# Attention scores over four banks, a block-diagonal state, and feed-forward units shifted by two, in a one-core transformer block

## The chip, the cores and the metric

The kernel runs on one core of a Trainium2 chip. The metric is device time in microseconds. In what follows PE is TensorE (PEld its weight loads), DVE is VectorE, ACT is ScalarE, POOL is GpSimd and SP is SyncE, which issues most of the transfers.

## The reference

One pre-norm block over 4096 tokens of width 256. Causal linear attention with 16 heads of 16, then a feed-forward part in which every one of 8 experts is computed for every token and weighted:

```python
x = x + attn(layernorm(x))        # q,k,v = x @ w_qkv; rope on q and k; q = elu(q*s)+1, k likewise
#   scan over tokens: kv += k v^T; ks += k; out = (q kv) / max(q . ks, 1e-6); then out @ w_out
x = x + ffn(layernorm(x))
#   inh = sigmoid(x @ Wr / temperature); weights w[token, expert] from it (a zone, else the two nearest)
#   h_e = silu(x @ Wg[e]) * (x @ Wu[e]);  out = sum_e w[:, e] * (h_e @ Wd[e])
```

## The kernel before, in words

Tokens go in 32 tiles of 128. Attention works a tile at a time (g), the feed-forward part a block of four tiles at a time (b, 512 tokens), in 16 units a block: unit n is one half (128 of 256 hidden columns) of one expert, so there are 128 units. To keep fp32 precision most operands are split into a high and a low part, and each product is made of three: hi·hi, hi·lo, lo·hi.

A tile's attention: `qkv` projects; ACT copies (`qk_copy`, `v_copy`); `cos` on DVE, two `sin` on POOL and `rope` make the rotation; `exp` and `phi` the feature map; `q_hi`, `k_hi`, `q_lo`, `k_lo` the split; SP transposes both. `scores(g, half)` makes 8 of the 16 heads' scores: a head takes 64 rows of the array, so an even and an odd head run as a pair into two banks, four heads to a bank. `mask` (DVE, four heads), `a_hi` (ACT) and `a_lo` (POOL) mask and split them; the masked scores have two buffers, so the third mask waits for the first `a_lo`. `av` adds, into two banks (even heads, odd heads), q times the running state (16 products of 64 rows and 51 columns, line 323) and then masked scores times v (32 products of 128 rows, line 330). `o_sum` adds the three parts of each bank, `norm` divides, `state` (line 341) and `st_add` update the running state, which `s1`, `st_rest`, `s2`, `s3` split in three. `o_T` transposes, `proj` projects, `x1_add` adds the residual, `bn2` to `ln2` normalise again, and `x2_T` transposes for the feed-forward part.

A unit: `gate` (6 products of 512 columns, bank G), `silu`, `up` (6, bank U), `h_up`, `h_hi`, `h_lo`, `down` (12 products of 256 columns into Y0 and Y1), and after each second unit four `acc`. Once a block `logit_rows` makes a 16 x 512 array of router rows, `lg_copy` brings it to SBUF, `logit` turns it to 128 x 32 with eight short products against `two` (line 407), and a chain of some 27 small DVE instructions (`route_*`) makes the weights.

The order on every engine is written out by hand: a prologue (tiles 0 to 4, steps 0 to 4), and then a loop over steps s from 5 (LAG). In a step, tile a = s has its `qkv` to `scores`, tile c = s - 1 its `av` to `x2_T`, and four units run, n = 4(s - 5) to n + 3; `down` runs two units later. An engine takes its instructions strictly in this order, and waits are on semaphores. Expert weights come in 24 slabs in the first steps (12 before step 5, four in each of steps 5, 6 and 7), each split by ACT and then by POOL or DVE.

The eight PSUM banks: G, U, Y0, Y1 for the units; R0 for q and k; R1 for v, `x2_T` and the logits; R2 and R3 for scores, then `av`, then `state` and `o_T`, `proj`. Since `scores`, `mask` and `av` share R2 and R3, the second half of the scores waits for the first half's masks.

Of the kernel before, what the change touches and what calls it, by code (L numbers as in the profile page):

```python
# [15 lines left out]
P = 128  # L16
# [22 lines left out]
LAG = 5  # L39
SLABS = 3 * E  # L40
# [3 lines left out]
STEPS = NTL + LAG + 1  # L44
# [24 lines left out]
def build(nc, x, xT, w_qkv, w_out, Wg, Wu, Wd, Wr, temperature, tab, out):  # L69
# [8 lines left out]
    with ctx:  # L78
# [32 lines left out]
        rop = sb("rop", [P, 2 * D])  # L111
# [27 lines left out]
        lg_rows = rt[0:2 * E, :, :, :].rearrange("p i t e -> p (i t e)")  # L139
        two = sb("two", [2 * E, E])  # L140
# [8 lines left out]
            for n in ("gate", "up", "y0", "y1", "front0", "front1", "back0", "back1"))  # L149
# [17 lines left out]
         s_onevx, s_two, s_zsx, s_zss, s_colmean, s_wc, s_wqkv_hi, s_wqkv_lo, s_wout_hi, s_wout_lo, s_wr_hi, s_wr_lo, s_slab_hi,  # L167
         s_slab_lo) = (sem(n) for n in (
             "ones", "mhalf", "mone", "rtemp", "rtemp2", "id0", "mask0", "id", "mask", "iota_i", "iota",
             "z_vx", "one_vx", "two", "z_sx", "z_ss", "colmean", "wc", "wqkv_hi", "wqkv_lo", "wout_hi", "wout_lo", "wr_hi", "wr_lo",  # L170
# [15 lines left out]
        ROUTE = ("inh", "off", "zone", "dist", "zone2", "m", "eq", "w0", "c", "ws", "ix", "no", "s1", "nd",  # L186
# [11 lines left out]
        def score_bank(g, r):  # L198
            return (G, Y1)[r % 2] if g < NT else BK[r % 2]
# [23 lines left out]
        logits = R1[:, D:D + NT * E].rearrange("p (t e) -> p t e", t=NT)  # L223
# [13 lines left out]

        def slab(s, i):

            if s < LAG:  # L240
                n = 3 * s + i
                return n if i < 3 and n < HEAD_SLABS else None
            n = HEAD_SLABS + STEP_SLABS * (s - LAG) + i
            return n if i < STEP_SLABS and n < SLABS else None
# [10 lines left out]
        def tensor_program(pe):  # L255
# [10 lines left out]
            def qkv(g):  # L266
# [23 lines left out]
            def scores(g, half):  # L290
# [5 lines left out]
                if half:  # L296
                    w.wait_ge(s_amask, 4 * g + 2)
                elif g < NT:
                    w.wait_ge(s_amask, 4 * g)
                else:  # L300
                    w.wait_ge(s_ss, 2 * g)
                    w.wait_ge(s_olo, g)
                    if g > NT:
                        w.wait_ge(s_x1, g)
                for j in range(4):
                    for odd in range(2):
                        rows = slice(64 * odd, 64 * odd + 64)
                        m = pe.matmul(score_bank(g, 2 * half + odd)[:, P * j:P * (j + 1)], kT[rows, 4 * half + j, :],  # L308
                                      qT[rows, g % 2, 4 * half + j, :], start=True, stop=True)
                m.then_inc(s_qk, 1)  # L310

            def av(g):
# [4 lines left out]
                w.wait_ge(s_s3, g)  # L317
                w.wait_ge(s_amask, 4 * g + 4)
# [8 lines left out]
                for odd in range(2):  # L327
                    for p in range(NP):
                        for a in a_p:
                            m = pe.matmul(BK[odd][:, p * WV:(p + 1) * WV], a[:, 2 * p + odd, :],  # L330
                                          vx[:, g % 2, 2 * p + odd, :, :].rearrange("p a b -> p (a b)"),
                                          start=False, stop=(p == NP - 1), skip_group_check=True)
                    m.then_inc(s_av, 1)
# [36 lines left out]
            def x2_T(g):  # L370
# [11 lines left out]
            def logit_rows(b):  # L382
# [15 lines left out]
            def logit(b):  # L398
# [59 lines left out]
            state(2); x2_T(1); scores(3, 0); o_T(2); scores(3, 1); proj(2); av(3); x2_T(2); state(3); o_T(3)  # L458
            proj(3); scores(4, 0); x2_T(3); scores(4, 1)
            for s in range(LAG, STEPS):  # L460
                a, c, n = s, s - 1, NT * (s - LAG)
                router = (s - LAG) // NT if (s - LAG) % NT == 0 else -1
                logit_rows(router); gate(n); qkv(a); up(n); logit(router); down(n - 2); av(c); gate(n + 1)
                up(n + 1); down(n - 1); state(c); o_T(c); gate(n + 2); proj(c); up(n + 2); gate(n + 3); down(n)
                scores(a, 0); x2_T(c); up(n + 3); down(n + 1); scores(a, 1)

        def scalar_program(act):
# [41 lines left out]
            def qk_copy(g):  # L509
# [3 lines left out]
                w.wait_ge(s_sin, 2 * g)  # L513
# [11 lines left out]
            def exp(g):  # L525
# [4 lines left out]
                act.activation(qk_bank(g)[:, :], rop[:, :], ACT.Exp, bias=mone[:, 0:1]).then_inc(s_exp, 1)  # L530
# [42 lines left out]
            def s1(g):  # L573
# [5 lines left out]
                act.activation(st_x[:, :, 0, :], st_s[:, :, :], ACT.Copy).then_inc(s_s1, 1)  # L579

            def s2(g):
# [3 lines left out]
                act.activation(st_x[:, :, 1, :], st_r[:, :, :], ACT.Copy).then_inc(s_s2, 1)  # L585
# [16 lines left out]
            def lg_copy(b):  # L602
                if not 0 <= b < NB:
                    return
                w.wait_ge(s_route, routed(b - 1, "wo"))
                w.wait_ge(s_lgrows, b + 1)
                act.activation(lg_rows[:, :], R0[0:2 * E, :], ACT.Copy).then_inc(s_lgc, 1)

            def th(b):
# [3 lines left out]
                w.wait_ge(s_logit, b + 1)  # L613
                act.activation(R["th"], logits, ACT.Tanh, scale=rtemp[:, 0:1]).then_inc(s_th, 1)
# [30 lines left out]
            wout_hi(); slab_hi(0); x_hi(1); qk_copy(0); v_copy(0); load_slab(1); exp(0); v1(0); k_hi(0); q_hi(0)  # L645
            qk_copy(1); v2(0); slab_hi(1); exp(1); slab_hi(2); x_hi(2); q_hi(1); k_hi(1); slab_hi(3); v_copy(1)
            a_hi(0, 0); v1(1); a_hi(0, 1); a_hi(0, 2); a_hi(0, 3); slab_hi(4); qk_copy(2); v2(1); v_copy(2); exp(2)
            s1(0); x_hi(3); v1(2); k_hi(2); q_hi(2); a_hi(1, 0); a_hi(1, 1); s2(0); o_hi(0); a_hi(1, 2); slab_hi(5)
            a_hi(1, 3); x_hi(4); slab_hi(6); qk_copy(3); v2(2); slab_hi(7); v_copy(3); s1(1); a_hi(2, 0); x2_hi(0)
            exp(3); s2(1); v1(3); a_hi(2, 1); o_hi(1); k_hi(3); q_hi(3); a_hi(2, 2); wr_hi(); a_hi(2, 3); v2(3)  # L650
# [628 lines left out]
```

## Time and profile before

| what | value |
|---|---|
| median of three runs | 815.7 us (815.56 to 816.89) |
| profiled execution: time | 815.4 us |
| profiled execution: span, first to last instruction | 813.5 us |
| PE busy | 769.8 us, 95% |
| DVE / ACT / POOL busy | 590.9 / 472.5 / 482.4 us, 73 / 58 / 59% |
| chain that ended last, share of PE | 92% |

Busy PE time counts each product from its start to its modelled end, and ends overlap the next start; the spacing of starts tells what a product costs. In the timeline, equal neighbouring instructions are merged into one row with a count.

### The profile page before, as it was taken

What the parts mean: (1) busy time and instruction counts of PE and PEld (TensorE: products, weight loads), DVE (VectorE), ACT (ScalarE), POOL (GpSimd) and SP (SyncE); (2) the same over time, 40 slices, a digit from 0 to 9 for tenths busy, and PEclk for the clock granted to TensorE, in tenths of its full rate; (3) what the DMA queues carried; (4) which work ended last, traced back from release to release, by engine and by line L of the source; (5) the groups of instructions that cost most, each with busy time, mean ns of one, the idle gap of its engine ahead of it and who ended that gap; (6) DMA issues with size and microseconds to landing.
All of it is one profiled execution on the core that took longest, in us unless ns stands there. A gap on an engine that the chain in (4) does not pass through costs nothing.

```text
span 813.5 us, 18123 instructions
## 1 busy us (share of the span) xinstructions
PE 769.8 (95%) x6696; PEld 658.1 (81%) x6696; DVE 590.9 (73%) x1587; ACT 472.5 (58%) x886; POOL 482.4 (59%) x537
## 2 busy tenths in 40 slices
PE   5375999999999999999999999999999999999997
PEld 3254688888888888888888888888888888888886
DVE  5788688868777787777766787777777787766333
ACT  2674776665656656655666556666656656634222
POOL 2786778755566576655666656565576555652332
PEclk9776899999999999999999999999999999999999
DMA  4545223122211022122201222120121121100000
GB/s 138 126 93 119 59 60 92 39 43 67 41 39 28 16 65 41 40 42 57 43 18 31 43 66 41 39 43 17 50 40 40 41 52 28 27 2 26 2 1 26
DMA packets 97319, 38.27 MB, mean 47 GB/s; under 512 B 74192, under 2 KB 96976, under 8 KB 97232
## 3 DMA queue, kind: packets, MB, share of 16 engines
q1 hardware_dynamic: 90704, 30.83, 17.6%
q10 hardware_dynamic: 6528, 6.29, 2.7%
q8 instruction: 53, 0.87, 0.4%
q14 instruction: 34, 0.28, 0.1%
HBM read 16.13 MB, written 4.19 MB: 25 GB/s over the span
## 4 chain that ended last, share of the span: by engine, by line
PE 92%; DVE 4%; ACT 1%; issue 1%; POOL 1%; DMA 0%; ACTq 0%; DVEq 0%; POOLq 0%
PE y L448 22%; PE gate L415 22%; PE up L415 22%; PE front L285 6%; PE back L330 3%; PE front L286 3%; PE back L366 2%; PE back L308 2%; PE back L341 2%; PE front L379 1%; PE back L353 1%; PE front L393 1%; PE back L323 1%; PE front L407 1%; POOL a_lo L1121 1%
## 5 line engine op out<-in xcount | busy, mean ns | idle before, releaser
L1149 POOL TENSOR_TENSOR h_lo<-work,h_hi 128x512 fp32r<-128x512 f32 x128 | 165.7, 1295 | 176.3 <-ACT h_hi L641 176.3
L1121 POOL TENSOR_TENSOR a_lo<-am,a_hi 128x512 f16<-128x512 f32 x120 | 140.2, 1180 | 67.4 <-ACT a_hi L570 67.1
L448 PE MATMUL y<-wd_hi,h_hi 128*128 128x256 f32 x512 | 145.0, 283 | 1.1 <-DVE xa L1024 1.1
L448 PE MATMUL y<-wd_lo,h_hi 128*128 128x256 f32 x512 | 143.0, 279 | 0.0
L448 PE MATMUL y<-wd_hi,h_lo 128*128 128x256 f32 x512 | 142.9, 279 | 0.0
L634 ACT ACTIVATE work<-gate 128x512 f32<-128x512 f32 x128 | 75.6, 591 | 81.4 <-PE gate L415 81.1
L1024 DVE SCALAR_TENSOR_TENSOR xa<-y,wo,xa 128x256 f32<-128x256 f32 x256 | 115.8, 471 | 7.8 <-PE y L448 7.6
L1012 DVE TENSOR_TENSOR work<-work,up 128x512 f32<-128x512 f32 x128 | 87.0, 680 | 36.2 <-PE up L415 31.8
L641 ACT ACTIVATE h_hi<-work 128x512 fp32r<-128x512 f32 x128 | 80.1, 626 | 48.5 <-DVE work L1012 31.6
L448 PEld LDWEIGHTS y<-wd_hi,h_hi 128*128 128x128 f32 x512 | 96.2, 188 | 8.2 <-issue 2.7
L797 DVE TENSOR_TENSOR am<-back,cmask 128x512 f32<-128x512 f32 x112 | 74.3, 684 | 38.0 <-PE back L308 37.9
L448 PEld LDWEIGHTS y<-wd_lo,h_hi 128*128 128x128 f32 x512 | 96.2, 188 | 4.7
L448 PEld LDWEIGHTS y<-wd_hi,h_lo 128*128 128x128 f32 x512 | 97.2, 190 | 0.0
L570 ACT ACTIVATE a_hi<-am 128x512 f16<-128x512 f32 x120 | 74.4, 628 | 35.3 <-DVE am L797 32.9
L415 PE MATMUL gate<-x_hi,wg_hi 128*128 128x512 f32 x256 | 87.7, 424 | 0.0
L415 PE MATMUL up<-x_hi,wu_hi 128*128 128x512 f32 x256 | 82.1, 402 | 0.0
L415 PE MATMUL gate<-x_hi,wg_lo 128*128 128x512 f32 x256 | 80.0, 394 | 0.0
L415 PE MATMUL up<-x_hi,wu_lo 128*128 128x512 f32 x256 | 79.7, 393 | 0.0
L415 PE MATMUL up<-x_lo,wu_hi 128*128 128x512 f32 x256 | 79.7, 392 | 0.0
L415 PE MATMUL gate<-x_lo,wg_hi 128*128 128x512 f32 x256 | 79.4, 391 | 0.0
L1100 POOL TENSOR_TENSOR rop<-qk,tabs 128x256 f32<-128x256 f32 x64 | 45.3, 728 | 25.3 <-ACT qk L515 25.3
L415 PEld LDWEIGHTS gate<-x_hi,wg_lo 128*128 128x128 f32 x256 | 48.4, 189 | 11.6
(194 smaller groups left out, 1654.1 us busy)
## 6 DMA issues: line engine op xcount, KB each, us to landing
xr<-xT SPq DMA_DIRECT2D x32, 128.0 KB, 2.5
xa<-x SPq DMA_DIRECT2D x32, 128.0 KB, 2.6
out<-xa SPq DMA_DIRECT2D x32, 128.0 KB, 1.8
xa<-Wg ACTq DMA_DIRECT2D x8, 256.0 KB, 2.9
work<-Wd ACTq DMA_DIRECT2D x8, 256.0 KB, 3.0
work<-Wu ACTq DMA_DIRECT2D x8, 256.0 KB, 2.9
work<-w_qkv SPq DMA_DIRECT2D x2, 384.0 KB, 3.7
qT<-q_st SPq DMA_TRANSPOSE x32, 3.2
```

Of the source, the lines that this page charges most:

```text
L285: pe.matmul(qk_bank(g)[:, :], lhs, wqkv_p[wi][:, k, 0:2 * D], start=first, stop=last)
L415: m = pe.matmul(ps, weights[wi][:, e_, k, m_ * P:(m_ + 1) * P], x2[xi][:, b % 2, k, :], start=(n == 0), stop=(n == 3 * KD - 1))
L448: m = pe.matmul(Y[t // 2][:, t % 2 * D:(t % 2 + 1) * D], h_p[hi][:, n % 2, t * P:(t + 1) * P], wd_p[wi][:, u // KI, u % KI, :], start=(n % ...
L570: act.activation(a_p[0][:, heads(r), :], am_place(g, r).rearrange("p (h n) -> p h n", h=4), ACT.Copy).then_inc(s_ahi, 1)
L634: act.activation(hb[:, n % 2, :], G[:, :], ACT.Silu).then_inc(s_g, 1)
L641: act.activation(h_p[0][:, n % 2, :], hb[:, n % 2, :], ACT.Copy).then_inc(s_hhi, 1)
L797: v.tensor_tensor(am_place(g, r).rearrange("p (h n) -> p h n", h=4), score_bank(g, r)[:, :].rearrange("p (h n) -> p h n", h=4), bcast(cmas ...
L1012: v.tensor_tensor(hb[:, n % 2, :], hb[:, n % 2, :], U[:, :], ALU.mult).then_inc(s_h, 1)
L1024: v.scalar_tensor_tensor(out=xs, in0=Y[t // 2][:, t % 2 * D:(t % 2 + 1) * D], scalar=wo[:, b % 2, t, e_:e_ + 1], in1=xs, op0=ALU.mult, op1 ...
L1100: pool.tensor_tensor(r2_h[:, :, half, :], qk_h[:, :, 1 - half, :], bcast(tabs[:, g // NT % 2, g % NT, at:at + HALF], 1, 2 * H), ALU.mult). ...
L1121: pool.tensor_tensor(a_p[1][:, heads(r), :], am_place(g, r).rearrange("p (h n) -> p h n", h=4), a_p[0][:, heads(r), :], ALU.subtract).then ...
L1149: pool.tensor_tensor(h_p[1][:, n % 2, :], hb[:, n % 2, :], h_p[0][:, n % 2, :].bitcast(F32), ALU.subtract).then_inc(s_hlo, 1)
```

## The change

- The scores of a tile use four banks, R0 to R3, and both halves run in one group. So `qkv(a)` of the next step waits for the first two masks, and `x2_T` moves one step later (to tile d = s - 2), between `up(n)` and `av(c)`.
- The units of a step are n = 4(s - 5) - 2 to n + 3: two fewer have run at a given tile. Steps 5, 6 and 7 are written out by hand (with ten units), the loop begins at step 8, and there is one more step at the end.
- The running state is kept block-diagonal by pairs of heads (its other blocks are zero, by a per-partition scale `own`), so q times the state is eight products of 128 rows and 102 columns. The state's buffers, and what `s1`, `st_rest`, `s2` and `s3` handle, have 272 columns for 136.
- `logit` is four transposes through the identity for eight products against `two`, and a new `route_sum` on DVE adds the two parts. `logit_rows` and `logit` go later in the step; the small routing instructions are split over two steps.
- `rope` writes over `qk`, so `qk_copy` waits for the `phi` of the tile before; the prologue's order is changed on all engines.

```diff
-            return (G, Y1)[r % 2] if g < NT else BK[r % 2]
+            return (G, Y1)[r % 2] if g < NT else (R0, R1, R2, R3)[r]
...
                 for p in range(NP):
-                    for odd in range(2):
-                        rows = slice(64 * odd, 64 * odd + 64)
-                        pe.matmul(BK[odd][:, p * WV:(p + 1) * WV], qT[rows, g % 2, p, :],
-                                  st_x[rows, p, :, :].rearrange("p a b -> p (a b)"),
-                                  start=(p == 0), stop=False, skip_group_check=True)
+                    pe.matmul(BK[p // 4][:, p % 4 * 2 * WV:(p % 4 + 1) * 2 * WV], qT[:, g % 2, p, :],
+                              st_x[:, p, :, :, :].rearrange("p h a b -> p (h a b)"),
+                              start=(p % 4 == 0), stop=False, skip_group_check=True)
...
                 for t in range(NT):
-                    m = pe.matmul(logits[:, t, :], lg_rows[:, t * P:(t + 1) * P], two[:, :], start=(t == 0),
-                                  stop=(t == NT - 1), skip_group_check=True)
+                    m = pe.transpose(R1[:, t * P:(t + 1) * P], lg_rows[:, t * P:(t + 1) * P], ident[:, :])
...
-            proj(3); scores(4, 0); x2_T(3); scores(4, 1)
-            for s in range(LAG, STEPS):
-                a, c, n = s, s - 1, NT * (s - LAG)
+            proj(3); scores(4, 0); scores(4, 1); x2_T(3); qkv(5); gate(0); av(4); up(0); o_T(4); state(4)
+            logit_rows(0); proj(4); gate(1); logit(0); scores(5, 0); gate(2); up(1); scores(5, 1); qkv(6); gate(3)
...
+            for s in range(FULL, STEPS):
+                a, c, d, n = s, s - 1, s - 2, NT * (s - LAG) - 2
                 router = (s - LAG) // NT if (s - LAG) % NT == 0 else -1
-                logit_rows(router); gate(n); qkv(a); up(n); logit(router); down(n - 2); av(c); gate(n + 1)
-                up(n + 1); down(n - 1); state(c); o_T(c); gate(n + 2); proj(c); up(n + 2); gate(n + 3); down(n)
-                scores(a, 0); x2_T(c); up(n + 3); down(n + 1); scores(a, 1)
+                qkv(a); gate(n); up(n); x2_T(d); av(c); gate(n + 1); down(n - 2); up(n + 1); state(c); o_T(c)
+                gate(n + 2); down(n - 1); proj(c); logit_rows(router); gate(n + 3); up(n + 2); logit(router)
+                down(n); scores(a, 0); scores(a, 1); up(n + 3); down(n + 1)
...
+                v.scalar_tensor_tensor(out=st_s[:, :, hh, :], in0=stp[:, :, hh, :], scalar=own[:, hh:hh + 1],
+                                       in1=st_s[:, :, hh, :], op0=ALU.mult, op1=ALU.add).then_inc(s_ss, 1)
...
+            def route_sum(b):
...
+                v.tensor_reduce(R["s2"], logits, AX.X, ALU.add).then_inc(s_route, 1)
```

The loop on DVE and ACT after the change, cut to what the prediction follows:

```diff
+                tcos_scale(a); mask(c, 2); route_first(late); mask(c, 3); acc(n - 4, 0); bn(a + 1); acc(n - 4, 1)
+                acc(n - 4, 2); acc(n - 4, 3); mean_var(a + 1); cos(a); route_second(late); o_sum(c, 0); rope(a)
+                x2_lo(d); o_sum(c, 1); h_up(n); den_max(c); den_rec(c); phi(a); var_eps(a + 1); route_tie(late)
+                norm(c); route_ix2(late); x_lo(a + 1); route_s2(late); k_lo(a); q_lo(a); o_lo(c); st_add(c)
...
+                acc(n - 2, 2); acc(n - 2, 3); bn2(c); mean_var2(c); var_eps2(c); h_up(n + 2); route_sum(router)
+                ln2(c); route_zone(router); route_nearest(router); route_weight(router); mask(a, 0); mask(a, 1)
+                h_up(n + 3)
...
+                a_hi(c, 2); x_hi(a + 1); a_hi(c, 3); v_copy(a); qk_copy(a); silu(n); h_hi(n - 1); x2_hi(d); exp(a)
+                silu(n + 1); k_hi(a); q_hi(a); h_hi(n); o_hi(c); v1(a); silu(n + 2); h_hi(n + 1); lg_copy(router)
+                s1(c); silu(n + 3); v2(a); th(router); s2(c); e1(router); h_hi(n + 2); fb(router); a_hi(a, 0)
```

## Rows read from the trace of the kernel before

**Rows 1.** The page: busy time by engine, and the chain that ended last.
```profile
PE 769.8 (95%) x6696; PEld 658.1 (81%) x6696; DVE 590.9 (73%) x1587; ACT 472.5 (58%) x886; POOL 482.4 (59%) x537
PE 92%; DVE 4%; ACT 1%; issue 1%; POOL 1%; DMA 0%; ACTq 0%; DVEq 0%; POOLq 0%
```

**Rows 2.** Windows: stretch, its length, busy us (instructions) by engine, granted clock, DMA share, GB/s.
```profile
0.00:100.00 100.00, 61.62 (x611) 46.51 (x612) 74.42 (x199) 58.02 (x117) 64.21 (x83) 0.78 0.44 106
...
100.00:125.00 25.00, 25.00 (x218) 21.61 (x217) 22.05 (x61) 17.36 (x33) 19.08 (x22) 1.00 0.40 87
...
300.00:400.00 100.00, 100.00 (x915) 86.26 (x914) 75.64 (x206) 62.05 (x114) 61.28 (x70) 1.00 0.18 39
```

**Rows 3.** Timeline of PE: start us, us, what; first product of qkv in two steps.
```profile
390.64 0.39 PE L285 MATMUL front<-wqkv_hi,xo_hi 128*128 128x512 f32 x1
...
413.56 0.39 PE L285 MATMUL front<-wqkv_hi,xo_hi 128*128 128x512 f32 x1
```

**Rows 4.** Timeline of PE: last product of down, av, first of gate.
```profile
395.42 0.28 PE L448 MATMUL y<-wd_hi,h_lo 128*128 128x256 f32 x1
395.63 0.38 PE L323 MATMUL back<-st_x,qT 64*128 64x51 bf16 x16
395.95 0.20 PE L330 MATMUL back<-vx,a_hi 128*128 128x51 bf16 x1
...
396.77 0.71 PE L415 MATMUL gate<-x_hi,wg_hi 128*128 128x512 f32 x2
```

**Rows 5.** Timeline of PE: last product of down, then state.
```profile
400.89 0.28 PE L448 MATMUL y<-wd_hi,h_lo 128*128 128x256 f32 x1
401.00 0.77 PE L341 MATMUL back<-vx,k_st 128*128 128x34 bf16 x24
```

**Rows 6.** Timeline of PE: x2_T into up; down into scores into gate.
```profile
408.56 0.44 PE L379 MATMUL front<-ident,nat 128*128 128x128 f32 x2
408.76 0.71 PE L415 MATMUL up<-x_hi,wu_hi 128*128 128x512 f32 x2
409.31 0.63 PE L415 MATMUL up<-x_hi,wu_lo 128*128 128x512 f32 x2
...
411.53 0.28 PE L448 MATMUL y<-wd_hi,h_lo 128*128 128x256 f32 x1
411.74 0.40 PE L308 MATMUL back<-qT,kT 64*128 64x128 f16 x8
412.07 0.74 PE L415 MATMUL gate<-x_hi,wg_hi 128*128 128x512 f32 x2
412.64 0.62 PE L415 MATMUL gate<-x_hi,wg_lo 128*128 128x512 f32 x2
413.10 0.62 PE L415 MATMUL gate<-x_lo,wg_hi 128*128 128x512 f32 x2
```

**Rows 7.** Timeline of PE in a router step: logit, then down.
```profile
369.90 1.05 PE L407 MATMUL front<-two,router 16*128 16x8 f32 x8
370.89 0.38 PE L448 MATMUL y<-wd_hi,h_hi 128*128 128x256 f32 x1
```

**Rows 8.** Timeline of all engines: masks, a_hi, a_lo and h_up.
```profile
408.75 1.29 DVE L797 TENSOR_TENSOR am<-back,cmask 128x512 f32<-128x512 f32 x2 [0.95 <-PE back L308]
...
409.47 1.23 ACT L570 ACTIVATE a_hi<-am 128x512 f16<-128x512 f32 x2
...
410.18 2.29 POOL L1121 TENSOR_TENSOR a_lo<-am,a_hi 128x512 f16<-128x512 f32 x2 [1.86 <-ACT a_hi L570]
...
410.50 0.69 DVE L1012 TENSOR_TENSOR work<-work,up 128x512 f32<-128x512 f32 x1
```

**Rows 9.** Timeline of DVE: rope, the two o_sum, after the av of rows 4.
```profile
395.79 0.69 DVE L772 SCALAR_TENSOR_TENSOR rop<-front,rop 128x512 f32<-128x512 f32 x1 [0.25 <-POOL rop L1100]
396.63 1.07 DVE L815 TENSOR_REDUCE osb<-back 128x136 f32<-128x408 f32 x2 [0.15 <-PE back L330]
```

**Rows 10.** Timeline of ACT: a table load ahead of exp.
```profile
394.42 1.28 ACT L530 ACT_TABLE_LOAD   x1
```

More of the change, by code:

```diff
@@ L612, in th @@
                 w.wait_ge(s_rtemp2, 1)
[L613 to L614 removed]
+                w.wait_ge(s_route, routed(b, "sum"))
+                act.activation(R["th"], R["s2"], ACT.Tanh, scale=rtemp[:, 0:1]).then_inc(s_th, 1)
             def e1(b):
@@ L654, in scalar_program @@
[L654 to L661 removed]
+            wout_hi(); x_hi(1); load_slab(1); slab_hi(0); qk_copy(0); v_copy(0); slab_hi(1); x_hi(2); v1(0); exp(0)
@@ L669, in setup_first @@
                 v.memset(mone[:, :], -1.0).then_inc(s_mone, 1)
+                for hh in range(2):
+                    for half in range(2):
+                        v.memset(own[64 * half:64 * half + 64, hh:hh + 1], ASCALE if half == hh else 0.0).then_inc(s_own, 1)
                 w.wait_ge(s_iota_i, 1)
@@ new lines, in vector_program @@
+            wout_lo(); tcos_scale(0); cos(0); rope(0); x_lo(1); phi(0); x_lo(2); tcos_scale(1); q_lo(0); k_lo(0)
+            slab_lo(2); rtemp_half(); cos(1); rope(1); phi(1); tcos_scale(2); mask(0, 0); mask(0, 1); q_lo(1)
+            mask(0, 2); k_lo(1); mask(0, 3); cos(2); o_sum(0, 0); o_sum(0, 1); rope(2); mask(1, 0); tcos_scale(3)
+            den_max(0); phi(2); st_add(0); den_rec(0); mask(1, 1); norm(0); x_lo(3); mask(1, 2); q_lo(2); k_lo(2)
+            mask(1, 3); o_lo(0); slab_lo(5); x1_add(0); bn2(0); cos(3); o_sum(1, 0); mean_var2(0); bn(4)
@@ new lines, in vector_program @@
+            var_eps2(0); o_sum(1, 1); mean_var(4); mask(2, 0); rope(3); den_max(1); ln2(0); den_rec(1); mask(2, 1)
+            norm(1); x_lo(4); wr_lo(); var_eps(4); phi(3); mask(2, 2); st_add(1); q_lo(3); tcos_scale(4); k_lo(3)
+            mask(2, 3); x2_lo(0); o_lo(1); cos(4); x1_add(1); slab_lo(8); bn2(1); o_sum(2, 0); o_sum(2, 1)
+            mean_var2(1); var_eps2(1); den_max(2); mask(3, 0); ln2(1); den_rec(2); st_add(2); norm(2); mask(3, 1)
+            x2_lo(1); rope(4); o_lo(2); mask(3, 2); mask(3, 3); phi(4); bn(5); x1_add(2); mean_var(5); bn2(2)
@@ new lines, in vector_program @@
+            mean_var2(2); var_eps2(2); k_lo(4); q_lo(4); o_sum(3, 0); ln2(2); o_sum(3, 1); den_max(3); den_rec(3)
+            norm(3); x_lo(5); x2_lo(2); o_lo(3); st_add(3); var_eps(5); x1_add(3); bn2(3); mean_var2(3); var_eps2(3)
+            mask(4, 0); tcos_scale(5); ln2(3); mask(4, 1); slab_lo(11); mask(4, 2); x2_lo(3); bn(6); mask(4, 3)
+            mean_var(6); cos(5); rope(5); phi(5); o_sum(4, 0); o_sum(4, 1); den_max(4); den_rec(4); slab_lo(14)
+            norm(4); q_lo(5); k_lo(5); o_lo(4); h_up(0); x1_add(4); bn2(4); x_lo(6); mean_var2(4); st_add(4)
@@ new lines, in vector_program @@
+            route_sum(0); var_eps2(4); slab_lo(17); var_eps(6); mask(5, 0); route_zone(0); mask(5, 1)
+            route_nearest(0); mask(5, 2); h_up(1); mask(5, 3); bn(7); route_weight(0); route_first(0); tcos_scale(6)
+            ln2(4); slab_lo(20); cos(6); o_sum(5, 0); h_up(2); rope(6); o_sum(5, 1); route_second(0); den_max(5)
+            mean_var(7); phi(6); den_rec(5); x2_lo(4); norm(5); x_lo(7); route_tie(0); h_up(3); route_ix2(0)
+            o_lo(5); q_lo(6); route_s2(0); k_lo(6); route_both(0); x1_add(5); route_out(0); var_eps(7); bn2(5)
@@ new lines, in vector_program @@
+            acc(0, 0); mean_var2(5); acc(0, 1); acc(0, 2); acc(0, 3); var_eps2(5); h_up(4); st_add(5); mask(6, 0)
+            mask(6, 1); h_up(5); mask(6, 2); ln2(5); tcos_scale(7); mask(6, 3); cos(7); acc(2, 0); acc(2, 1)
+            rope(7); acc(2, 2); h_up(6); acc(2, 3); o_sum(6, 0); bn(8); o_sum(6, 1); phi(7); mean_var(8); den_max(6)
+            acc(4, 0); den_rec(6); norm(6); q_lo(7); h_up(7); k_lo(7); slab_lo(23); o_lo(6); acc(4, 1); acc(4, 2)
+            acc(4, 3); st_add(6); var_eps(8); h_up(8); x1_add(6); x2_lo(5); mask(7, 0); bn2(6); mean_var2(6)
```

214 lines of the change are left out of this document (100 added, 114 removed).

## The prediction

> **What bounds the kernel now.** I read the page first: PE is busy for 95% of the span, and 92% of the chain that ended last is PE's own work [rows 1]. Then the windows: from 100 us on PE is busy in every microsecond at the full clock (1.00, 2.4 GHz), while DVE has 76% and ACT and POOL about 62% in the middle of the run; in the first 100 us PE is busy for only 61.6 us at a mean clock of 0.78 [rows 2]. So there are two regimes. After the prologue the time is the sum of what PE issues, and work taken from another engine is worth nothing; a step lasts 413.56 - 390.64 = 22.92 us [rows 3]. In the prologue PE waits for the others. "Busy" hides PE's small losses, as products overlap in the record. The timeline shows them as spacings: a pair of 512-column products takes 0.46 us (412.64 to 413.10), 0.23 each [rows 6], and a down product is normally followed after 0.11 to 0.12 us [rows 5].
>
> **The change part by part, on PE.**
>
> *Entries.* Where down is followed by 64-row products the spacing is 0.21 us in place of 0.12: before the state products of av [rows 4] and before each half of the scores [rows 6]. Before `state`, which has 128 rows and the same type as av's products, it is 0.11, so nothing is lost [rows 5]. The change makes av's first products 128-row ones (0.09 gone) and puts both halves of the scores in one group (another 0.09).
>
> The Trainium skill's page "TensorEngine Tiling (Array Packing)", section Key Properties, says that a change of the tiling mode, not of the tile, drains the engine; by this rule, the trace agrees: these 0.09 us are that drain, and they stand only before 64-row groups.
>
> *Exits.* After a group of short products the first pair of 512-column ones takes longer, their weights not being loaded under anything: 0.57 against 0.46 after scores, 0.55 after x2_T [rows 6]. With one group of scores one exit goes (0.11), and with x2_T put just before av, which ends in such an exit anyway, another goes (0.09).
>
> *State products.* Sixteen take 395.95 - 395.63 = 0.32 us [rows 4]. At one column a cycle of 2.4 GHz eight of 102 columns take 8 x 0.0425 = 0.34; I take +0.05 with the entry from x2_T. Bounds: the 32 v products behind them go at (396.77 - 395.95) / 32 = 0.026 us each [rows 4]; if the wide ones went so too, 0.21, a gain of 0.11. A product of x2_T takes 0.10 [rows 6]; at that price 0.80, a loss of 0.48 a tile.
>
> The same page, section Performance Considerations, wants two-way row tiling for a contraction of 64 or less, which speaks against this edit: two tiles side by side would take 51 columns a pair, 8 x 0.021 = 0.17 us (an estimate from its rule), and undoing them would cost 0.17 a tile, 5.4 us over 32. The row says 0.32 before, 0.04 a pair, so the pairs do not get their columns for half; the row decides.
>
> Sum for a tile: -0.09 - 0.09 - 0.11 - 0.09 + 0.05 = -0.33. Tiles 4 to 31 are in the PE-bound part: 28 x 0.33 = 9.2 us.
>
> *Router.* Eight products against `two` last 370.89 - 369.90 = 0.99 us [rows 7], with a drained entry (they have 16 rows; I take the 0.09 of rows 4). Four transposes of x2_T's kind take 4 x 0.10 = 0.40 [rows 6]; the exit stays. -0.68 a block, eight blocks: 5.4 us. Bounds: 4 x 0.09 above, and nothing gained below, if a transpose took the 0.25 of two such products.
>
> **Waits, one step of the new order.** They are what can eat this. Let T be the start of the scores; widths from rows 4, 6, 8 and 9.
>
> *Masks to av.* Mask 0 starts at T + 0.5, as before [rows 6, 8], a mask each 0.64, a_hi 0.62, a_lo 1.14: a_lo 0 ends at 3.1, a_lo 1 at 4.2. The third and fourth mask wait for these two buffers, so mask 3 ends at 4.9, its a_hi at 5.5; POOL has `s3` (0.44 in the old width, I take double) and a_lo 2 until 6.1, and a_lo 3 until 7.3. PE comes to av after scores 0.65, up 1.5, down 1.4, qkv 6 x 0.23 + 6 x 0.12 = 2.1, gate and up 2.8, x2_T 0.2: T + 8.6. Spare: 1.3 us. qkv at T + 3.6 waits for masks 0 and 1, done at 1.9: spare 1.7.
>
> *av to up(n+1).* Queued on DVE are o_sum 0, rope, x2_lo, o_sum 1, h_up. With A the start of av: o_sum 0 at A + 1.0 (396.63 - 395.63) [rows 4, 9], 0.53 each, rope 0.62, x2_lo some 0.4 (half of h_up's columns), h_up 0.65: A + 3.7. PE is at up(n+1) at A + 1.14 + gate 1.5 + down 1.4 = 4.0. Spare: 0.3 us, the smallest of all. norm, behind phi, ends at A + 5.2, and o_T comes at 6.1.
>
> *Router steps.* The routing stands in front of the masks: route_sum 0.7 us after up(n+2) ends, tanh, then e1 behind a table load of 1.28 us [rows 10], so that mask 0 starts some 3.4 us after up(n+2), 1.0 later than the scores would allow. It leaves 0.3 of the 1.3. And exp is called between two silu, so two more loads, 2.6 us of ACT, one of them before silu(n); gate(n+1) has about 0.9 us for that. I take 0 and keep 1 us a block as a bound.
>
> The Trainium skill's page "ScalarE: Activation LUTs", section "Table sets: the hidden batching unit", puts a load at about 2.7 us (its section on the cost itself at 1.28); at 2.7 silu(n) would come 1.4 later and a router step stall by half a microsecond or more. The row of this case, 1.28, decides.
>
> *The wider state.* s1, s2, st_rest, s3 handle twice the columns: at most double, under 1 us together, with 14 us between `state` and the av that needs them. st_add has as many columns as before over more partitions. route_sum and the second half of the routing lie in DVE's free quarter. All at nothing; if that cover went, DVE would be the bound and each would count.
>
> **Prologue and steps 5 to 7.** Here PE is not alone. qkv(5) now runs before the router rows of block 0, in a gap, worth up to 1 us. But ten units are run by step 8 for twelve. The three steps, 68.8 us now, hold six groups of 1.4 us less (two gates, ups and downs) and savings of 1.7, and the router rows of block 0 (0.9) come in: about 59.5 us of PE. DVE had between 76% (an ordinary step) and 88% (22.05 of 25 us) of such a time [rows 2], 52 to 60 us; less two h_up and four acc, 3 us, it is 49 to 57 us for PE's 59.5, 83 to 97%. ACT and POOL have the slabs on top too. With every engine so full PE must wait somewhere. Whatever is lost here is paid in full, as the two postponed units run at the end. I take +3.4 us, bounds -2 and +9. Tiles 0 to 3 are reordered on all engines with the same work; DVE carries 74 of the first 100 us [rows 2]. I take 0, bounds -4 and +4.
>
> **Sum.** -9.2 - 5.4 + 3.4 = -11.2 us. The profiled execution took 815.4 us, span 813.5, within 0.3 of the median of 815.7, so the sum is made on the median: 804.5 us.
>
> **The rivals.**
>
> *A. The head eats more.* Steps 0 to 7 lose 9 us for 3.4. For: the loads above, and 38 us of PE idle before 100 us, where any order matters. Against: PE hardly idled after 100 us although DVE was at 88%. 810.
>
> *B. The small losses move and do not vanish.* Entries and exits turn out to be per group of products whatever their rows, and the wide products cost 0.1 more than thought: tile gain 0.1, 2.8 us, router 5.4, head +3.4. For: x2_T to av is a pair that the trace never shows. Against: rows 5. 811.
>
> *C. Router steps stall.* e1 and the added loads hold masks and silu up past their spare, 1.5 us in each of seven blocks: +10.5. For: DVE waits for ACT there with the masks behind it. Against: the spares. 815, no change.
>
> *D. Slower: up(n+1) waits for h_up(n) in every step.* DVE's five instructions between av and up have 0.3 us to spare. If x2_lo waits for x2_hi (behind a_hi, two copies, silu and h_hi on ACT), or rope for sin, DVE stops with h_up behind it and PE with it. Beyond 0.3 us late each 0.1 costs 2.8 us over 28 tiles; it decides from 0.3 + 11.2 / 28 = 0.7 us late. At 1.2 late: 28 x 0.9 = 25, so 829. For: a DVE at three quarters has only a quarter to catch up with. Against: x2_T ends at A and DVE comes to x2_lo only at A + 2.1; the sins start when qk is copied, long before.
>
> **How the numbers follow.** Forecast 0.60, A 0.14, B 0.10, C 0.07, D 0.09. A measurement of this kernel tells 0.2%, 1.6 us, from no change. Forecast, A and B are faster, and a little of C: 0.86; same 0.04 (C); slower 0.10 (D and C's tail). The forecast's own range is 799 to 808 (bounds of wide products, router and head); with A, B and most of C it is 797 to 815.
>
> **What would show it.** In the trace after: av's first eight products start 0.1 after x2_T's last and take 0.34 to 0.36; one group of 16 score products in 0.65; the transposes of the logits in 0.4; steps of 22.6 us with no PE idle in the middle; idle of PE between 80 and 140 us some 4 us. Wrong would be: PE idle before up, av or gate in every step (D, C), a step still near 22.9 (B), or PE idle for over 8 us between 80 and 140 us (A).

## The result, and the profile after

The changed kernel takes 828.3 us (827.4 to 829.2, four runs) against 815.6 us (815.1 to 816.9) for the kernel before: ratio 1.0153, interval 1.0135 to 1.0171. It is slower by 12.7 us, where 804.5 was forecast and 797 to 815 was the range. The profiled execution took 827.7 us, its span 826.0.

The page of the changed kernel, busy time and chain, answers to [rows 1]:

```profile
PE 771.7 (93%) x6408; PEld 661.0 (80%) x6408; DVE 613.3 (74%) x1598; ACT 504.5 (61%) x898; POOL 494.2 (60%) x538
PE 81%; POOL 5%; DVE 4%; ACT 4%; issue 3%; DMA 2%; SPq 0%; ACTq 0%; DVEq 0%; POOLq 0%
```

PE issues 288 products fewer and is busy for longer. The windows of [rows 2]:

```profile
0.00:100.00 100.00, 61.03 (x549) 46.37 (x550) 73.77 (x185) 56.04 (x112) 66.78 (x84) 0.73 0.44 110
100.00:125.00 25.00, 18.94 (x139) 15.05 (x137) 20.19 (x53) 17.39 (x30) 14.43 (x16) 0.93 0.26 69
300.00:400.00 100.00, 99.03 (x864) 85.79 (x863) 80.43 (x217) 68.50 (x120) 64.25 (x71) 1.00 0.19 39
```

From 100 to 125 us, where PE had no gap before, it is now busy for 18.9 of 25 us. From 80 to 140 us it is busy for 48.0 of 60 us (57.0 before): 12 us idle, where the forecast named 4 and its rival A over 8. In the middle it is nearly full again. The two timelines of PE that the forecast rested on, scores and x2_T to av, answer to [rows 4, 6]; the first row is the last down product ahead of the scores:

```profile
411.70 0.27 PE L436 MATMUL y<-wd_hi,h_lo 128*128 128x256 f32 x1
411.91 0.40 PE L302 MATMUL front<-qT,kT 64*128 64x128 f16 x8
412.14 0.39 PE L302 MATMUL back<-qT,kT 64*128 64x128 f16 x8
412.46 0.73 PE L403 MATMUL up<-x_hi,wu_hi 128*128 128x512 f32 x2
413.03 0.63 PE L403 MATMUL up<-x_hi,wu_lo 128*128 128x512 f32 x2
413.50 0.63 PE L403 MATMUL up<-x_lo,wu_hi 128*128 128x512 f32 x2
...
420.30 0.38 PE L371 MATMUL front<-ident,nat 128*128 128x128 f32 x2
420.51 0.54 PE L316 MATMUL back<-st_x,qT 128*128 128x102 bf16 x8
420.89 0.18 PE L323 MATMUL back<-vx,a_hi 128*128 128x51 bf16 x1
...
421.72 0.71 PE L403 MATMUL gate<-x_hi,wg_hi 128*128 128x512 f32 x2
```

The structure is the forecast's: one group of scores, entered after 0.21 us and 0.55 long (0.65 was forecast); the wide state products 0.38 long; no gap before av. But the pairs of 512-column products stand 0.47 apart, not 0.46. Averaged from 160 to 700 us, the spacing of such pairs is 0.4664 us (0.4599 before) and that of down products 0.1194 (0.1166). Nothing in the code of those products was changed.

The first `qkv` product of two steps, for [rows 3]; the step between them, 23.53 us, is the one behind a router step:

```profile
391.87 0.39 PE L276 MATMUL front<-wqkv_hi,xo_hi 128*128 128x512 f32 x1
...
415.40 0.40 PE L276 MATMUL front<-wqkv_hi,xo_hi 128*128 128x512 f32 x1
```

Ordinary steps take 22.85 us (22.92 was forecast to become 22.6), a block of four 93.4 (93.8). PE's waits from 150 to 740 us (what waited, for what; us, times, longest), of which there were none before, and the largest of those from 60 to 160 us:

```profile
PE gate L403 <- ACT work L628: 2.9, 6, 0.5
PE back L323 <- POOL a_lo L1142: 0.4, 1, 0.4
...
PE y L371 <- DVE nat L895: 4.3, 3, 3.1
PE back L323 <- POOL a_lo L1142: 3.7, 3, 1.6
PE gate L403 <- ACT work L628: 3.1, 2, 2.8
PE y L359 <- DVE ox_lo L859: 2.7, 3, 1.1
PE front L302 <- DMA kT<-k_st: 1.9, 1, 1.9
```

Divided at the first product of `qkv(8)` and of `qkv(31)`, in us; what lies before `qkv(8)` is called the head below. At `qkv(8)` the changed kernel has run seven groups (gate, up or down of a unit) fewer, 1.4 us each; I count these 9.8 us, which fall behind `qkv(31)`, to the head:

| stretch | forecast | changed less before |
|---|---|---|
| to qkv(8) (155.1, now 158.0) | +1.4 | 2.9 + 9.8 = +12.7 |
| 23 steps (539.8, now 537.6) | -11.7 | -2.2 |
| tail (118.6, now 130.4) | -1.0 | 11.8 - 9.8 = +2.0 |
| span (813.5, now 826.0) | -11.3 | +12.5 |

The forecast's column is its own terms laid out: four tiles, a router and the 3.4 in the first stretch, 23 tiles and six routers in the second, one of each in the tail.

Both large terms are off: 11 us in the head, 12.5 in everything after it.

### The profile page after: what moved, and what is told of

It reads as the page before. It is cut to its first block, busy times and chain, and to the rows that moved or that the text cites. A ratio compares the mean times of both kernels' runs of the same rounds, so it can differ in the third digit from the quotient of the medians.

```text
span 826.0 us, 17554 instructions
## 1 busy us (share of the span) xinstructions
PE 771.7 (93%) x6408; PEld 661.0 (80%) x6408; DVE 613.3 (74%) x1598; ACT 504.5 (61%) x898; POOL 494.2 (60%) x538
## 4 chain that ended last, share of the span: by engine, by line
PE 81%; POOL 5%; DVE 4%; ACT 4%; issue 3%; DMA 2%; SPq 0%; ACTq 0%; DVEq 0%; POOLq 0%
PE y L436 21%; PE gate L403 21%; PE up L403 20%; PE front L276 5%; POOL a_lo L1142 3%; PE back L323 3%; PE front L277 2%; PE back L359 2%; PE back L334 2%; DMA kT<-k_st 1%; PE front L302 1%; PE back L346 1%; PE back L316 1%; PE front L384 1%; ACT qk L508 1%
## 5 line engine op out<-in xcount | busy, mean ns | idle before, releaser
L1031 DVE SCALAR_TENSOR_TENSOR xa<-y,wo,xa 128x256 f32<-128x256 f32 x256 | 109.9, 474 | 30.1 <-PE y L436 30.1
L403 PE MATMUL gate<-x_hi,wg_hi 128*128 128x512 f32 x256 | 85.8, 416 | 6.6 <-ACT work L628 6.6
L816 DVE TENSOR_REDUCE osb<-back 128x136 f32<-128x408 f32 x64 | 36.7, 575 | 34.0 <-PE back L323 34.0
L403 PEld LDWEIGHTS gate<-x_lo,wg_hi 128*128 128x128 f32 x256 | 48.3, 189 | 11.8
```

Of the source, the lines that this page charges most:

```text
L403: m = pe.matmul(ps, weights[wi][:, e_, k, m_ * P:(m_ + 1) * P], x2[xi][:, b % 2, k, :], start=(n == 0), stop=(n == 3 * KD - 1))
L816: v.tensor_reduce(osb[:, 8 * half:8 * half + 8, :], BK[half][:, 0:8 * WV].rearrange("p (h s d) -> p h d s", s=3, d=W1), AX.X, ALU.add).the ...
L1031: v.scalar_tensor_tensor(out=xs, in0=Y[t // 2][:, t % 2 * D:(t % 2 + 1) * D], scalar=wo[:, b % 2, t, e_:e_ + 1], in1=xs, op0=ALU.mult, op1 ...
```

## Experiments

Theory: the head pays for the postponed units in full, and the middle loses its gain because products are issued at a wider spacing, x2 (what gate and up read) and h (what down reads) standing at other addresses (x2 at 193216 bytes of a partition for 193344, h at 220320 for 220480). Rival for the middle: the new order itself. First the kernel before again, for a second trace, beside the changed kernel with its old addresses, one part alone, and all parts without the shift.

> The kernel before, unchanged, traced again, to compare product spacings. Between the two traces gate and up pairs of 512 columns went from 0.460 to about 0.467 us and down products from 0.1184 to 0.1199 (means). Placement theory: this kernel has 0.460 and 0.118 again, on whichever chip. Chip theory: it shows 0.467 and 0.120 where a copy of the changed kernel would.

816.9 us, span 815.1; `qkv(5)` at 87.7 and `qkv(8)` at 156.6 (86.3 and 155.1 in the first trace), so single traces differ by 1.5 us in the head, and ordinary steps by nothing (22.8 to 22.9 in both). Its pairs are 0.460 apart and its down products 0.117, as in the first trace, so the wider spacing isn't a matter of which execution was traced.

**e1_pad: the changed kernel, x2 and h at the addresses of before.**

```diff
-        own = sb("own", [P, 2])
+        own = sb("own", [P, 34])
...
+        gap = sb("gap", [P, 8])
         wo = sb("wo", [P, 2, NT, E])
```

> The changed kernel with 128 unused bytes per partition ahead of xa and 32 ahead of wo, so that xa, x2, the router array, work and h lie at the addresses of the kernel before; order and work unchanged. Placement theory: pairs return to 0.460 and down products to 0.118; 768 pairs x 0.0065 + 1536 x 0.0015 = 7 us less than 828.3, so 821 (ratio to before about 1.007). Rival (chip, or the new order itself): spacing stays at 0.467 and 0.120, ratio 1.015.

821.4 us, ratio 1.0060 (1.0046 to 1.0075): 6.9 us less than the changed kernel (7.6 by the ratios), with not one instruction changed. Its gate and up rows at the same place as above are 0.46 apart:

```profile
412.96 0.62 PE L404 MATMUL gate<-x_hi,wg_hi 128*128 128x512 f32 x2
413.42 0.62 PE L404 MATMUL gate<-x_hi,wg_lo 128*128 128x512 f32 x2
413.88 0.62 PE L404 MATMUL gate<-x_lo,wg_hi 128*128 128x512 f32 x2
414.34 0.62 PE L404 MATMUL up<-x_hi,wu_hi 128*128 128x512 f32 x2
```

Ordinary steps take 22.59: the gain of a tile, 0.29, was there and had been covered. The new order as the cause of the wide spacing is out. A block gains 1.33, not 4 x 0.33 + 0.68; the wait of gate for silu stands in its trace too (3.5 us in six steps, each the one behind a router step).

**e2_logit: the transposed logits and route_sum in the kernel before, nothing else.**

```diff
-                    m = pe.matmul(logits[:, t, :], lg_rows[:, t * P:(t + 1) * P], two[:, :], start=(t == 0),
-                                  stop=(t == NT - 1), skip_group_check=True)
+                    m = pe.transpose(R1[:, t * P:(t + 1) * P], lg_rows[:, t * P:(t + 1) * P], ident[:, :])
```

> The kernel before with one part of the change: logits by four transposes and a route_sum, in the place where logit stood. Step theory (each edit is worth what I forecast, the loss is in the order of the first eight steps): logit takes 0.4 for 0.99 us and a drained entry, 8 x 0.68 = 5.4 us, so 810.3. Rival (the routing chain is what counts): the extra DVE instruction ahead of tanh delays exp or h_up, and the gain stays under 2 us: 814.

811.5 us, ratio 0.9938 (0.9926 to 0.9950), -5.1 by the ratio; a router step takes 23.54 for 24.31. The size was right.

**e3_all and e4_parts: all parts but the shift, in two orders.** Logits, block-diagonal state and scores over four banks. In e3 `logit_rows` runs in the step before and the whole routing stands ahead of `x2_lo`:

```diff
+                route_s2(router); route_both(router); route_out(router); x2_lo(c)
+                slab_lo(slab(s, 3)); h_up(n + 3); mask(a, 0); mask(a, 1)
```

> The kernel before, its prologue, its units (not shifted) and its order, with all three parts on PE: transposed logits, block-diagonal state, both score halves in one group over R0 to R3; x2_T stays in its step, ahead of up(n+3), and buffers lie as before. Theory 1 (the loss is in the prologue and steps 5 to 7): per tile -0.09 -0.09 -0.11 +0.05 = -0.24, 28 tiles 6.7 us, router 5.4, the head as before: 815.6 - 12 = 804, range 801 to 808. Theory 2 (one score group over four banks makes the steps wait: masks to av has little to spare): PE idle before av or qkv in every step, 815 or more.

822.9 us, ratio 1.0079 (1.0066 to 1.0092): a miss by 19 us. Ordinary steps took 22.57, router steps 25.4 for 24.3. PE's waits from 150 to 740 us name it:

```profile
PE front L412 <- ACT vs L534: 5.6, 6, 0.9
PE front L382 <- DVE router L1004: 2.8, 6, 0.5
PE front L313 <- DVE x_lo L919: 1.0, 6, 0.2
```

`logit` waited for v's copy out of the bank that they share, `x2_T` for routing. In e4 the rows go to bank U at the start of the step, and `route_both` and `route_out` come last:

```diff
+                route_s2(router); x2_lo(c); h_up(n + 3); mask(a, 0); mask(a, 1)
+                slab_lo(slab(s, 3)); route_both(router); route_out(router)
```

> The three parts again on the prologue, units and buffers of the kernel before, with the routing mended: the router rows go to bank U at the start of the step (free there), so no score group waits for them, and x2_lo and the masks stand ahead of the last routing instructions. In the run e3_all the ordinary steps were 22.57 us for 22.86 of before and the router steps 25.4 for 24.3. Parts theory (the edits are worth 0.3 a tile and 4.3 us of routing; the changed kernel lost them elsewhere): 815.7 - 28 x 0.3 - 4.3 = 803. Rival (four banks for one tile's scores cost waits whatever the order): PE idle in router steps stays, 812 or more.

809.8 us, ratio 0.9914 (0.9901 to 0.9928). Ordinary steps take 22.57; the expectation of 803 missed 0.4 us in each step behind a router step (down for acc, which waits for the late `route_out`: 1.4 us in 7 in its trace) and 2.7 in the head.

**e5_shift: e4 with the units shifted by two**, stores and loads as in the changed kernel.

```diff
-SHIFT = 0
+SHIFT = -2
...
-                a, c, n = s, s - 1, NT * (s - LAG)
+                a, c, n = s, s - 1, NT * (s - LAG) + SHIFT
```

> e4_parts with one thing more: the units of a step are n = 4(s-5)-2 to n+3 from step 5 on, and one more step at the end; the order in a step, the prologue and the buffers are those of e4_parts. Shift theory: in steps 5 to 7 the kernel before had little PE idle, so two units (8.4 us of gate, up and down) put off there are paid in full at the end: e4_parts + 6 to 8.5. Order theory (the hand-written order of steps 5 to 7 is what costs): the shift alone costs under 3 us.

819.4 us, ratio 1.0035 (1.0022 to 1.0047). By the medians the shift alone costs 9.65 us, no less than two units at the end. The two traced executions differ by only 6.6 us (e4's lies 2.6 above its median): there e5 comes to `qkv(8)` 1.9 us earlier, with 8.4 us of units not yet run. So the head gives back little or nothing. From 60 to 160 us, e4 and then e5 (for the kernel before the same window has 88.73 of PE, for the changed one 81.75):

```profile
60.00:160.00 100.00, 88.25 (x781) 73.83 (x780) 77.52 (x207) 64.42 (x122) 74.22 (x79) 0.87 0.36 78
```

```profile
60.00:160.00 100.00, 82.63 (x739) 68.07 (x738) 78.95 (x205) 61.21 (x119) 72.00 (x77) 0.86 0.34 77
```

PE does 5.6 us less in the same time, while DVE is busy for 77.5 and 79.0. In e5 two of PE's waits in that window have grown, `av` for a_lo from 1.4 us and `state` for o_sum from 0.8:

```profile
PE back L330 <- POOL a_lo L1134: 3.3, 2, 1.9
PE back L341 <- DVE osb L821: 3.0, 2, 2.1
```

The granted clock is lower in the head too, which the forecast didn't count. From 60 to 120 us it is 0.83 of 2.4 GHz in the kernel before and 0.74 in the changed one (0.78 in e4, 0.77 in e5):

```profile
60.00:120.00 60.00, 48.73 (x510) 39.07 (x501) 48.06 (x139) 39.50 (x77) 42.91 (x48) 0.83 0.35 84
```

```profile
60.00:120.00 60.00, 41.92 (x401) 32.57 (x402) 45.63 (x110) 35.04 (x69) 43.13 (x47) 0.74 0.38 94
```

In the changed kernel the clock even falls once more after it had come up: PE was busy for 15.15 of the 24 us from 89 to 113, waited 2.85 us for a silu, and then had 0.51 of the clock from 113.0 to 116.4. Over the whole head (to `qkv(8)`), 44.4 and 51.2 us lie at 1.2 GHz in the two traces of the kernel before, 54.6 in e4, and 58.0 in each of e5, e1_pad and the changed kernel. What this costs, no run separates. The two traces of the kernel before are 6.8 us apart in it and 1.5 us apart at `qkv(8)`; at that rate (an estimate) the 7 to 14 us more of the changed kernel are 1.5 to 3 us of its head.

**e7_state: the block-diagonal state alone, in the kernel before.**

```diff
-                    for odd in range(2):
-                        rows = slice(64 * odd, 64 * odd + 64)
-                        pe.matmul(BK[odd][:, p * WV:(p + 1) * WV], qT[rows, g % 2, p, :],
+                    pe.matmul(BK[p // 4][:, p % 4 * 2 * WV:(p % 4 + 1) * 2 * WV], qT[:, g % 2, p, :],
```

> The kernel before with the block-diagonal state alone (rope into qk, wider st_s, st_r, st_x; addresses from xa on unchanged). av's first eight products take 0.38 us for sixteen in 0.32, with the entry of 0.21 us back at 0.12: 32 x -0.03 = -1 us, 814.7. Rival: the wider s1, st_rest, s2, s3 and the qk buffer shared with rope slow the prologue, where the others bound: 817 or more.

816.8 us, ratio 0.9999 (0.9990 to 1.0008): no change, where 1 us less was expected.

**Addresses, in the kernel before.** Six runs move buffers and change no instruction. e6: 32 unused bytes ahead of wo. e8: den and rec (128 bytes) go from ahead of nat to behind h. e11: to behind x2. e12, e13: 128 and 256 unused bytes ahead of nat. e14: 128 ahead of wo. The edits are of this kind (e8, e14):

```diff
-        den = sb("den", [P, H])
-        rec = sb("rec", [P, H])
...
         h_p = [sb(f"h_{s}", [P, 2, B], F32R) for s in ("hi", "lo")]
+        den = sb("den", [P, H])
+        rec = sb("rec", [P, H])
```

```diff
+        gap = sb("gap", [P, 32])
         wo = sb("wo", [P, 2, NT, E])
```

> The kernel before with 32 unused bytes per partition ahead of wo, so that work and h (not x2) lie 32 bytes further, as h does modulo 64 in the changed kernel. Placement theory, the part of h: down products go from 0.118 to 0.120 and gate and up stay at 0.460; +2 to +4 us, 818 to 819. If the whole effect sits in x2, or in distances other than modulo 64: no change, 815.7.

> The kernel before with one edit: the two small buffers den and rec (128 bytes a partition together) are allocated behind h in place of ahead of nat, so that everything from nat to h stands 128 bytes lower: x2 exactly where the changed kernel has it, h still on a multiple of 64 bytes. No instruction changes. Theory (the spacing of products depends on the address of their operand, x2's for gate and up, h's for down): pairs of gate and up 0.466 us for 0.460 in the middle of the run, down products unchanged at 0.116 to 0.117, and with 768 pairs (128 units, 6 pairs each) about +4 to +5 us, ratio 1.005. Rival (only the 32-byte offset of h and its neighbours matters, or what was seen in the changed kernel is owed to its order): 816, pairs 0.460.

> The kernel before with den and rec allocated right behind x2: x2 (and what stands between nat and it) 128 bytes lower, at 193216, work and h where they were. Theory (each product's spacing depends on the address of its own operand): pairs of gate and up 0.466 us as in the run with everything 128 bytes lower, down products back at 0.1166 (there 0.1179); 768 pairs at +0.006 = +4.6 us less what is idle anyway: about 820. Rival (what counts is h's or work's address, or the mere sum of what moved): pairs 0.460 and 816, or pairs and down both slow and 821.

> The kernel before with an unused buffer of 128 bytes ahead of nat: x2 at 193472, h at 220608, both 128 bytes higher. If the pattern of fast and slow addresses repeats every 256 bytes, this is the same as 128 bytes lower: pairs 0.466, down 0.118, about 821. If only the distance or the order counts (lower is slow, higher not): 816 and 0.460.

> The same with 256 bytes: x2 at 193600, h at 220736. If the pattern repeats every 256 bytes: pairs 0.460, down 0.1166, 816, as the kernel before. If every other address than that of before is slow: 821.

> The kernel before with 128 unused bytes ahead of wo: wo, work and h 128 bytes higher (h at 220608), x2 where it was. With x2 alone lower by 128, the pairs went to 0.4665 and the down products to 0.1148. If the pairs follow x2's own address and the down products the distance between x2 and h (odd in units of 128 bytes is good): pairs 0.460, down 0.115, 1536 x 0.0017 = 2.6 us less: about 814, ratio 0.997. Rival (down follows h's own address, 220608 as in the run with everything 128 bytes higher): down 0.118 and 818 to 819, pairs 0.460.

Bytes moved, mean spacing of pairs of gate and up and of down products between 160 and 700 us (some 320 and 990 of them each), ratio to the kernel before with interval:

| run | x2 | h | pair | down | ratio |
|---|---|---|---|---|---|
| before | 0 | 0 | 0.4599 | 0.1166 | 1 |
| e6_align | 0 | +32 | 0.4592 | 0.1182 | 1.0025 (1.0015, 1.0036) |
| e14_h128 | 0 | +128 | 0.4610 | 0.1178 | 1.0019 (1.0010, 1.0028) |
| e11_x2only | -128 | 0 | 0.4666 | 0.1148 | 0.9997 (0.9988, 1.0006) |
| e8_x2addr | -128 | -128 | 0.4666 | 0.1179 | 1.0052 (1.0038, 1.0066) |
| e12_g128 | +128 | +128 | 0.4666 | 0.1179 | 1.0062 (1.0049, 1.0076) |
| e13_g256 | +256 | +256 | 0.4609 | 0.1164 | 1.0001 (0.9992, 1.0010) |
| changed | -128 | -160 | 0.4664 | 0.1194 | |
| e1_pad | 0 | 0 | 0.4613 | 0.1156 | |

With x2 the buffers from nat on move too, and with h wo and work; but of these the pairs read x2 alone, and the down products h. The pairs are at 0.459 to 0.461 with x2 at 0 and +256, at 0.4665 with it at -128 and +128, wherever h is. The down products are slow with h moved by 32 or 128, and as before at 256. The expectation of e14, that the distance of the two decides, fell, its rival held. Two more missed: e8's down products were to stay as they were, and e11 was to cost 4 us. In e11 the down products are quicker than ever, and over the 20 steps behind `qkv(8)` they give back 1.7 of the 2.1 us that gate and up lose; why is not settled. Nor is h's address all that sets the down products: with x2 and h where they stood, they take 0.1156 in e1_pad and 0.1157 in e10, for 0.1166 before. The rows of e11's pairs, and of e14's:

```profile
412.53 0.63 PE L415 MATMUL gate<-x_hi,wg_lo 128*128 128x512 f32 x2
413.00 0.63 PE L415 MATMUL gate<-x_lo,wg_hi 128*128 128x512 f32 x2
413.46 0.39 PE L285 MATMUL front<-wqkv_hi,xo_hi 128*128 128x512 f32 x1
```

```profile
415.16 0.63 PE L416 MATMUL gate<-x_hi,wg_lo 128*128 128x512 f32 x2
415.63 0.62 PE L416 MATMUL gate<-x_lo,wg_hi 128*128 128x512 f32 x2
```

One row tells little at a resolution of 0.01; the mean over hundreds does, and the modelled durations (0.62 or 0.63) show nothing.

**A version that beats both.** e4's parts, with the first half of the routing back ahead of `x2_lo`; e9 leaves the block-diagonal state out, e10 has it, e15 is e10 with h 128 bytes higher.

```diff
-                route_s2(router); x2_lo(c); h_up(n + 3); mask(a, 0); mask(a, 1)
-                slab_lo(slab(s, 3)); route_both(router); route_out(router)
+                route_s2(router); route_both(router); x2_lo(c); h_up(n + 3); mask(a, 0); mask(a, 1)
+                slab_lo(slab(s, 3)); route_out(router)
```

> Meant to beat both kernels: the kernel before with transposed logits and four-bank scores, without the block-diagonal state and without the shift; on DVE the first half of the routing stays ahead of x2_lo, h_up(n+3) and the masks, and route_out comes after the masks. From earlier runs: an ordinary step gains 0.3 (of that 0.09 was to come from av's entry, which stays, and 0.05 is not paid), router 4.35, the prologue pays nothing as the state edit that made qkv(5) a microsecond later is out. 28 x 0.25 + 4.35 = 11: about 806. Rival (the 0.3 of a tile needs the state edit): 816 - 4.35 - 28 x 0.15 = 808. Rival (the late route_out holds acc and down in the step after a router step, 0.4 each as in the version with all three parts, and the head loses 2.7 as there): 811.

> The same with the block-diagonal state as well: differs from the version of the three parts run earlier only in that the first half of the routing is ahead of x2_lo. If the wait of that version (down for acc for route_out) goes: 809.8 - 7 x 0.4 = 807, ordinary steps 22.57. Beside e9 it says what the state edit is worth in this order: the forecast's terms give -0.09 + 0.05 a tile, 28 x 0.04 = -1.1; alone it gave 0. Rival (state costs a microsecond in the prologue): e9 + 1.

> The fastest version so far (transposed logits, four-bank scores, block-diagonal state, no shift; 0.9872 of before) with the same 128 bytes ahead of wo. There the down products already take 0.1157 with h at 220480. If the distance decides as in e14_h128: 0.115 or a little less, ratio 0.985 or 0.986. Rival: 0.118, ratio 0.990.

e9: 808.6 us, ratio 0.9890 (0.9876 to 0.9903); e10: 806.6, ratio 0.9872 (0.9858 to 0.9885); e15: 809.9, ratio 0.9922 (0.9909 to 0.9936), its down products at 0.1176 for 0.1157. e9 was expected at 806; its rivals named 808 and 811. In e15 the rival of the distance theory came out in the spacing (0.118), while the ratio lies just above its 0.990. By the ratios e10 is 22.9 us quicker than the changed kernel. Its steps take 22.57, 22.57, 23.49 and 23.44, and PE waits for 1.1 us from 150 to 740:

```profile
PE front L379 <- DVE router L994: 0.5, 1, 0.5
PE y L450 <- DVE xa L1036: 0.4, 1, 0.4
PE front L379 <- DVE nat L900: 0.2, 1, 0.2
```

## Why the prediction was wrong

**The gain of a tile held.** Forecast 0.33 us; 0.29 in e1_pad, 0.29 to 0.33 in e4 and e10. The entries went as worked out: one of 0.21 for the scores, and x2_T straight into av. The wide state products took 0.38, against 0.34 to 0.36. The exits were counted wrong, and the total came right by luck. In the kernel before, the first half of the scores did not run into 512-column products but into x2_T, so a step had four exits (after av, after o_T, after x2_T, after the second half of the scores):

```profile
408.24 0.40 PE L308 MATMUL back<-qT,kT 64*128 64x128 f16 x8
408.56 0.44 PE L379 MATMUL front<-ident,nat 128*128 128x128 f32 x2
```

The changed kernel has three, so one exit goes and not two. In place of the other, the group of scores itself is 0.1 us shorter than two halves of 0.33, which the forecast had left at 0.65.

**The router's gain was right by itself and mostly lost in place.** Forecast 0.68 a block. In e2 a router step gains 0.77 and the kernel 5.1 us. In the changed order, addresses undone, a block gains 1.33, of which 4 x 0.29 is the tiles': 0.17 is left. The forecast saw where: "one of them before silu(n); gate(n+1) has about 0.9 us for that. I take 0 and keep 1 us a block as a bound." PE waits 0.5 us there in the step behind the router step, and that step is 0.7 us longer than its neighbours (23.53 for 22.85; 23.37 for 22.59 in e1_pad, where the whole of it stands between av and gate). On ACT that silu stands behind the a_hi of the fourth mask, for which ACT itself waited, two copies and a table load:

```profile
395.31 0.63 ACT L563 ACTIVATE a_hi<-am 128x512 f16<-128x512 f32 x1 [0.74 <-DVE am L798]
395.85 0.46 ACT L516 ACTIVATE vs<-front,rstd 128x256 f32<-128x256 f32 x1
396.20 0.68 ACT L508 ACTIVATE qk<-front,rstd 128x512 f32<-128x512 f32 x1
396.90 1.28 ACT L628 ACT_TABLE_LOAD   x1
398.20 0.60 ACT L628 ACTIVATE work<-gate 128x512 f32<-128x512 f32 x1
```

The forecast had set the load against a spare worked out with nothing late.

**The step that failed: "Prologue and steps 5 to 7 ... I take +3.4 us, bounds -2 and +9."** The forecast took 9.3 us out of PE's 68.8 in steps 5 to 7 (six groups and the savings, less the router rows), and had PE wait for a part of it. It reckoned with shares of busy time (83 to 97% for DVE), said itself that PE must wait somewhere, and still priced the waits at 3.4 us only. The runs show that these steps don't get shorter at all: from `qkv(5)` to `qkv(8)` the changed kernel takes 73.2 us for 68.8, and 69.7 in e1_pad. The shift by itself costs 9.65 us by the medians (e5 over e4): two units of 12 x 0.23 + 12 x 0.12 = 4.2 us are 8.4, and a little more. PE's waits there are for single results of DVE, POOL and ACT in the chain of a tile, though none of these engines is full. In e1_pad the stretch to `qkv(8)` costs 9.3 by the count of the table (156.1 for 156.6, and 9.8), and as the forecast set 2.0 of savings in it, the term measures 11.3 for 3.4, outside its bound of 9. It may be larger: against the first trace of the kernel before it is 12.8, and the traced execution of e1_pad is 3.1 us under its median. A part of it, not separated, is the lower clock. By itself the 11.3 would have given 812, still in the range.

**What no step had: the addresses.** +6.9 us (e1_pad). "The sum of what PE issues" took 0.23 and 0.12 us for constants of the products; they belong to a layout. The wider state, the buffers `rop` and `two` gone and `own` added moved x2 and h. All rivals of the prediction were waits or counts of products; none was of this kind.

In parts of the median, by the ratios: parts -7.0 (e4), shift +9.9 (e5 over e4), addresses +7.6 (changed over e1_pad), and 2.0 for the rewritten order with its silu wait (e1_pad over e5, hardly clear of the noise): +12.5.

**The rivals.** D named 829 and the time is 828.3. That is chance, not its mechanism: no up waited for h_up in any step. A (the head eats more) was true, at 11.3 for its 9. C happened at about half its size (0.7 us a block for 1.5). B did not.

## What to carry to other kernels

Where PE is full, look at the mean spacing of products that the change does not touch, before and after: if it has moved, look for buffers that have moved with it, and pad until the hot operands stand where they stood (here a move by 256 bytes did no harm). Work that was postponed out of this prologue was paid in full; before counting on less, look for a trace that shows PE alone setting the time there, as shares of busy time under 100% don't. And move small chains such as the routing one instruction at a time: the same parts gave 822.9, 809.8 and 806.6 us in three orders.

## What was not expected of the hardware

- The spacing of products depends on the address of the activations they read: 0.460 or 0.4665 us for two of 512 columns by x2's address, and for one of 256, by h's, 0.1166 or 0.118 in the same order (0.1148 in e11). In the moves tried, 256 bytes on both buffers change nothing and 128 on both cost 4 to 5 us of 816. Of 128 bytes on one, h's cost 1.6 us (e14) and x2's nothing (e11), so the times don't add up. The cause isn't known; the weights stood still in all of these runs.
- Eight 128-row products of 102 columns (0.38 us) are worth no more than sixteen 64-row ones of 51 with their slow entry (0.32 and 0.09): the change of form gained nothing (e7), or at most 0.2%, e10 over e9, whose intervals overlap.
- The time of the kernel before goes with its mean granted clock from execution to execution: thirteen at 0.972 took 815.0 to 815.8 us, sixteen at 0.966 took 816.7 to 818.1. In the two traced ones the difference lies in the head, where PE waits.
